# Another score bank for the softmax normalization, and activation loads issued from ScalarE's queue beside transposing DMAs, in a fused attention and feed-forward layer

## The reference, cut to what matters

```python
xn = layernorm(x)
qkv = xn @ w_in + b_in;  q, k, v = split into 16 heads
scores = q @ k.T / 8 + alibi_bias          # slope per head, causal
out = softmax(scores) @ v @ w_out + b_out
# feed-forward with quantized activations (127 / max|row|) and ternary weights
gate = silu(actq(xn) @ wq(w_gate).T);  up = actq(xn) @ wq(w_up).T
ffn  = actq(gate * up) @ wq(w_down).T
return x + out + ffn
```

## Time and profile before

| | us |
|---|---|
| timed runs, lowest / median / highest (2 runs) | 2321.36 / 2351.29 / 2381.23 |
| the profiled execution, total | 2316.97 |
| its span on the slowest core (core 0) | 2315.4 |
| spans of the eight cores | 2290.6 to 2315.4 |
| PE busy (share of the span) | 1431.2 (62%) |
| VectorE busy | 1009.0 (44%) |
| ScalarE busy | 755.1 (33%) |
| mean granted TensorE clock, core 0 | 0.775 |

### The profile page before, as it was taken

One profiled execution on the slowest core, in us unless ns is written; L12 is line 12 of the kernel. 1 busy time (PEld: TensorE's weight loads), 2 busy tenths in 40 slices (PEclk: granted clock), 3 DMA queues, 4 the chain that ended last, 5 costly groups with the idle time before them and its releaser, 6 DMA issues.

```text
span 2315.4 us, 22641 instructions; the slowest of 8 cores (2290.6 to 2315.4 us)
## 1 busy us (share of the span) xinstructions
PE 1431.2 (62%) x5304; PEld 510.8 (22%) x5304; DVE 1009.0 (44%) x1639; ACT 755.1 (33%) x1150; POOL 163.5 (7%) x276
## 2 busy tenths in 40 slices
PE   0004444466746565755657641859999999409998
PEld 0001111111211111111112110314444444204443
DVE  3005677464466763345674430215555555401110
ACT  0662222456644446756455540011221111000000
POOL 2000111100001110001110000100000000000000
PEclk9997666756657675666667665879999999759999
DMA  4764555332334453424551019781101000295661
GB/s 147 238 214 151 177 164 165 126 113 88 106 99 141 134 146 107 144 79 133 148 156 51 18 22 195 234 202 33 46 37 46 37 37 37 64 205 126 153 160 55
DMA packets 277092, 274.25 MB, mean 118 GB/s; under 512 B 208226, under 2 KB 224738, under 8 KB 276964
## 3 DMA queue, kind: packets, MB, share of 16 engines
q1 hardware_dynamic: 256740, 205.68, 34.9%
q0 software_dynamic: 20224, 67.12, 7.7%
HBM read 155.32 MB, written 67.11 MB: 96 GB/s over the span
## 4 chain that ended last, share of the span: by engine, by line
PE 42%; DVE 22%; DMA 10%; ACT 9%; issue 8%; SPq 6%; DVEq 1%; POOL 0%; ACTq 0%; POOLq 0%
PE pb L914 9%; PE pb L831 8%; PE pb L809 8%; DVE fa L529 7%; ACT ba L583 6%; SPq L189 6%; PE pb L448 5%; PE pb L503 4%; DMA fa<-w_gate 3%; DVE ba L770 3%; PE pb L570 2%; DMA s_acc<-fa 2%; DVE ba L730 2%; DVE ba L732 2%; DVE ba L735 2%
## 5 line engine op out<-in xcount | busy, mean ns | idle before, releaser
L583 ACT ACTIVATE ba<-pb,fa 128x512 bf16<-128x512 f32 (+2 forms) x522 | 338.9, 649 | 261.7 <-PE pb L570 217.8
L503 PE MATMUL pb<-ba 128*65 128x512 bf16 x502 | 232.1, 556 | 178.2 <-DVE ba L597 128.5
L759 PE MATMUL pb<-ba 128*128 128x512 bf16 x256 | 92.1, 525 | 298.9 <-DVE ba L360 173.3
L914 PE MATMUL pb<-ba 128*128 128x512 bf16 x992 | 221.2, 381 | 84.7 <-DMA ba<-s_n 84.7
L529 DVE RECIPROCAL fa<-fa 1x512 f32<-1x512 f32 x64 | 213.8, 3341 | 49.7 <-ACT fa L524 44.4
L570 PE MATMUL pb<-ba 64*128 64x512 bf16 (+2 forms) x502 | 134.7, 503 | 158.7 <-DVE ba L544 157.6
L831 PE MATMUL pb<-ba 128*128 128x512 bf16 x896 | 215.7, 381 | 23.0 <-DMA ba<-s_mu 23.0
L809 PE MATMUL pb<-ba 128*128 128x512 bf16 x896 | 216.3, 382 | 9.6 <-DVE fa L795 9.6
L819 ACT ACTIVATE fa<-pb,fa 128x512 f32<-128x512 f32 x128 | 87.9, 687 | 363.1 <-PE pb L813 363.1
L841 DVE SCALAR_TENSOR_TENSOR fa<-pb,fa 128x512 f32<-128x512 f32 x128 | 96.1, 751 | 157.9 <-PE pb L835 157.5
L914 PEld LDWEIGHTS pb<-ba 128*128 128x128 bf16 x992 | 97.5, 98 | 203.4 <-issue 87.6
(11 more groups left out here) (101 smaller groups left out, 1321.2 us busy)
## 6 DMA issues: line engine op xcount, KB each, us to landing
fa<-w_gate SPq DMA_DIRECT2D x64, 512.0 KB, 5.1
fa<-w_up SPq DMA_DIRECT2D x64, 512.0 KB, 3.9
fa<-w_down SPq DMA_DIRECT2D x64, 512.0 KB, 4.2
fa<-x SPq DMA_DIRECT2D x48, 512.0 KB, 6.1
s_n<-ba POOLq DMA_DIRECT2D x32, 512.0 KB, 2.9
fa<-w_in SPq DMA_DIRECT2D x24, 512.0 KB, 6.7
s_mg<-ba POOLq DMA_DIRECT2D x32, 256.0 KB, 5.3
s_mu<-ba POOLq DMA_DIRECT2D x32, 256.0 KB, 4.3
```

Of the source, the lines that this page charges most:

```text
L503: g = B.op("tensor", lambda e, ob=B.P[obank], k=ki2, hh=h2, pb=pbuf2, f1=first, l1=lastk: e.matmul(ob[0:65, :], v_sb[:, 1040 * k + 65 * hh ...
L583: eg.append(B.op("scalar", lambda e, b=Sb, q=qg0, g0=gw, a=wlo, c=col, pb=pbuf, jj=j: e.activation(out=pb[:, q - 512 * jj:q - 512 * jj + g ...
L759: B.em("tensor", lambda e, b=Pb, cc=c, t=ts_, hh=half: e.matmul(b[:], xn_fm[cc][:, 128 * t:128 * t + 128], wv_sb[:, 1024 * cc + 512 * hh:1 ...
L914: B.em("tensor", lambda e, b=Pb, cc=c, lt=tl, hh=half, nf=n2f: e.matmul(b[:], nf[cc][:, 128 * lt:128 * lt + 128], md[cc][:, 512 * hh:512 * ...
```

## The change

There are three parts.

1. `part2` takes the third bank of the head's pool (4 or 7) and no longer the first (2 or 5).
2. In the output projection the 16 loads of x are issued from ScalarE's queue, with the same gates. In the down projection the 16 loads of `s_acc` are, too.
3. In the down projection the first transpose of `s_n2` is issued before that of `s_md`. That of `s_md` is split into chunks 0 to 15 and 16 to 31, and PE waits for the second only before the 17th matmul of the first half tile.

```diff
@@ part2 @@
-                        rbank = SPOOL[loc3][0]
+                        rbank = SPOOL[loc3][2]
@@ ph_outproj @@
-            dv = B.dma("sync", xt[par], xv[t], "LX%d" % par, gate=ld_guard[par])
+            dv = B.dma("scalar", xt[par], xv[t], "LX%d" % par, gate=ld_guard[par])
@@ ph_ffn_down @@
-        dtr = B.dma("sync", md_all.rearrange("p (c t) -> p c t", c=NO),
-              B.s_md.rearrange("t (c p) -> t c p", c=NO), "DTR", transpose=True,
-              gate=B.gateup_tail + B.mdone.get("d", []) + t_f2 + s_f2)
-        B.waitg("tensor", [dtr])
...
         load_n2(0)
+        dtr_gate = B.gateup_tail + B.mdone.get("d", []) + t_f2 + s_f2
+        dtr_a = B.dma("sync", md_all.rearrange("p (c t) -> p c t", c=NO)[:, 0:16, :],
+                      B.s_md.rearrange("t (c p) -> t c p", c=NO)[:, 0:16, :], "DTR",
+                      transpose=True, gate=dtr_gate)
+        dtr_b = B.dma("sync", md_all.rearrange("p (c t) -> p c t", c=NO)[:, 16:32, :],
+                      B.s_md.rearrange("t (c p) -> t c p", c=NO)[:, 16:32, :], "DTR2",
+                      transpose=True)
+        B.waitg("tensor", [dtr_a])
...
-                dv = B.dma("sync", acc[par], av[t], "LA%d" % par, gate=ld_guard[par])
+                dv = B.dma("scalar", acc[par], av[t], "LA%d" % par, gate=ld_guard[par])
...
                     for c in range(NO - 1):
+                        if tg_ == 0 and tl == 0 and half == 0 and c == 16:
+                            B.waitg("tensor", [dtr_b])
```

## The result

The changed kernel takes 2306.9 us (median of 28 runs, 2275.9 to 2409.9) against 2317.1 us for the kernel before beside it (27 runs). The ratio is 0.9915, 95% interval 0.9896 to 0.9935: faster by 0.85%, less than the 2% that counts as a change, and outside the forecast range (2240, 2205 to 2292). The profiled execution took 2292.4 us, its slowest core 2290.8 us. Executions in which the cores of one die show a lower granted clock than the others are left out of the ratios, which is why 0.9915 is not 2306.9 / 2317.1, and of such a profile only the other die's cores are read; without them the changed kernel's median is about 2298, still outside the range.

What follows compares the result with a forecast made beforehand. Bounded by feed-forward matmuls, by waits among PE, ACT and DVE in the attention, and by transposing DMAs in the holes. 2317 - 40 (bank) - 36 (x loads) - 2 (down projection) = 2239, say 2240 us; range 2205 to 2292.

Steps and rivals of the forecast that it cites:

- The check on L570's waits: Attention: PE's score matmul waits for the normalization's multiply (L544) should fall from 157.6 us to roughly 110.
- Rival 2: Attention: the bank change gives nothing, as DVE's backlog fills the moved waits; total 2279 us, chance 0.11.
- step (a): Output projection's tile loop: two tiles per cycle, 11.9 us with a 9.7 us store landing; 8 cycles end at 1483.
- step (b): Output projection's DMA engines: 32 plain transfers cost the transposes 1.2 us each, 38 in all; end 1488 to 1489, gain 36.
- Rival 1: Output projection: ACT's loads get through only after the transposes are handed over; total 2275 us, chance 0.17.
- Rival 3: Output projection: loads cost the transposes nothing, both hide in each other; total 2215 us, chance 0.12.
- Rival 4: Output projection: transposes break down among 4 KB rows, 6 us per transfer; total 2389 us, slower, chance 0.05.
- SP held over 120 us by the two: Output projection: the transposes of s_n and s_mg holding SP over 120 us would show rival 4.
- the step: Down projection: s_acc loads beside the last s_n2 store delay the transposes up to 2.5 us, taken as 1.5.
- PE's two waits for s_md: Down projection: PE starts about 2060, does 16 matmuls, idles 15 us, then waits for s_md's second half until 2081.
- the second wait: Down projection: PE's second wait at L914 ends within 2 us of the old distance from the last s_n2 store.
- slices 24 and 36: Profile page's slices: the two places where TensorE was read as low, outside the feed-forward matmuls and the attention.

Runs made afterwards that it cites:

- e1_bank: Kernel before with only the normalization's move to bank 2 of the pool, all loads staying on SP's queue: 2272.3 us, ratio 0.9812.
- i0_before_one: Kernel before, unchanged, launched on one core alone instead of eight: 2257.5 us in one execution.
- e4_bank_down: Changed kernel with only the output projection's x loads put back on SP's queue: 2272.0 us, ratio 0.981.
- i1_one_core: Changed kernel launched on one core alone instead of eight: 2209.9 us in one execution.
- k2_two_halves: Changed kernel with each x load and s_acc store of the output projection issued as two half-row transfers: 2279.9 and 2291.5 us, too few for a ratio.
- h1_four_cores: Changed kernel launched on cores 0, 2, 4 and 6 alone instead of all eight: 2291.4 us.
- h2_x_later_sp: Changed kernel with x loaded and added in the down projection, s_acc and x loads on SP's queue, second s_n2 transpose behind two tiles' loads: 2232.9 us, ratio 0.9616.

## Why the prediction was wrong

**Part 1: right.** Taken 40 us; measured 41.3 in the changed kernel, and 1.9% or 43.6 us in e1_bank, with signs and places as worked out. The check on L570's waits (roughly 110) was too low, 123.7; the rest of the gain came from waits behind it (L503's for L597), which the prediction didn't list. Rival 2 falls.

**Part 2, step (a): right about the cycle.** DVE's adds on core 5, the tile pairs 13 us apart where 11.9 were forecast:

```profile
1416.79 1.48 DVE L669 TENSOR_TENSOR fa<-fa,pb 128x512 f32<-128x512 f32 x2 [10.69 <-DMA s_acc<-fa]
...
1429.88 1.48 DVE L669 TENSOR_TENSOR fa<-fa,pb 128x512 f32<-128x512 f32 x2 [9.59 <-DMA s_acc<-fa]
```

**Part 2, step (b): the step that failed**, "So a transfer costs the transposes 1.2 us; 32 of them [...] cost 38". It was mis-sized in three ways. The 1.2 us came from one store beside one transpose; with all of them there a store costs 1.7 and a load 2.2. On the quick cores that comes to 55 us instead of 38: the transposes hold SP 116 us instead of 103, and the output projection takes 122 instead of 107 (143 - 36), a gain of 14 against the mean of before. Second, one lone transfer couldn't show what both kinds do in full density on two neighbouring cores: in most pairs one of the two falls, here by a further 57 us on average. Why is open. Third, the sum was made for one core as if it stood for eight; the time is that of the worst of them.

**Rivals.** Rival 1 (loads starve) falls: x landed in 10.8 and 17.7 us beside the transposes. Rival 3 (both free) falls on every core. Rival 4 had the mechanism: its sign, "SP held over 120 us by the two", is there on cores 1, 2, 4 and 7 at 167.5 to 179.6. Its price was (173.1 - 61) / 32 = 3.5 us per transfer on these, averaged over all 32, just short of the 3.75 from which it decides, and far from the 6 it was worked out with. It deserved more than 0.05: the only row against it was a single store.

The Trainium skill's rule that was weighed, that spreading DMAs over issuing engines saves only issuing time ("DMA: Bandwidth & Descriptors", section "Issuing engines are not separate DMA queues"), gave 2275 for a part 2 worth nothing. Without part 2 the kernel takes 2272.0, and with it 24 us more. The rule warned in the right direction; that moving the issue may cost is what the runs add.

The Trainium skill's page "HBM Reference", section "Specifications (TRN2)", says that two cores share a memory domain's bandwidth, and that a DMA-bound change is to be measured with the pair active. The advice agrees with i0_before_one (8 MB in 29.6 us alone, 38.1 to 43.6 with the neighbour). Its rate of about 358 GB/s per core was reached by none of the stretches with transposes that were read here (279 GB/s the most, on one core alone), and the parted cores 4 and 5 moved 385 to 416 together, so a limit at that rate is not what they ran into.

**Part 3: right in being small**, 2 us forecast, +0.2% of time measured alone and nothing beside part 1 (e4_bank_down against e1_bank). The last s_n2 store landed late, as the step said, but by more. PE's two waits for s_md came as described, but closer together (10.0 us idle between them, where 15 was worked out):

```profile
2002.59 0.53 POOL L191 DMA_DIRECT2D s_n<-ba  x1 [5.04 <-DVE fa L877]
...
2010.40 15.28 SPq L189 DMA_TRANSPOSE ba<-s_n  x1
2025.97 30.86 SPq L189 DMA_TRANSPOSE ba<-s_md  x2
2043.23 5.80 PE L920 MATMUL pb<-ba 128*128 128x512 bf16 x15 [57.35 <-DMA ba<-s_md]
2059.05 6.20 PE L920 MATMUL pb<-ba 128*128 128x512 bf16 x15 [10.02 <-DMA ba<-s_md]
```

The transposes start 7.8 us after the store's issue; before it was 2016.60 - 2012.43 = 4.2, so 3.6 lost where 1.5 was taken. One sign was wrong: the second wait should have ended within 2 us of the old distance from the last s_n2 store (2081.13 - 2012.43 = 68.7), and ended 2059.05 - 2002.59 = 56.5 us after it, 12 us sooner. The next paragraph has the reason.

**What gave part of it back.** The down projection is 281.1 us in the changed kernel and 292.5 in e4_bank_down, with the same code from the barrier on. In the changed kernel the spans of a pair's cores up to it differ by some 50 to 70 us, and the first 12 MB of its transposes hold SP 15.28 + 30.86 = 46 us (46 to 48 on all eight cores), as on a lone core (14.89 + 31.04 = 45.9 in i1_one_core); where the cores reach it about together, in e4_bank_down, they take 54 to 62, the most on core 0:

```profile
1974.28 20.21 SPq L189 DMA_TRANSPOSE ba<-s_n  x1
1994.78 41.91 SPq L189 DMA_TRANSPOSE ba<-s_md  x2
```

That the distance in time is the cause fits i0_before_one (down projection 282.2 without a neighbour), and k2_two_halves shows it within one execution of one kernel: its parted pairs 2/3 and 4/5 hold SP 46 to 48 us there and have a down projection of 280.8 to 282.7, its other two pairs 54 to 61 and 288.9 to 299.1. It wasn't tried by itself. So a pair that doesn't part gains little over the whole kernel: in the 16 executions of the changed kernel, the mean span of a pair's two cores is 2257.9 us where they differ by 45 us or more and 2263.6 where they differ by under 26. What the parting costs is that the time is that of the slower one. For the slowest cores of the two profiles, core 4 after and core 0 before, the account closes: attention -45.3, output projection +41.6 (185.0 against 143.4), gate and up -2.5, down -18.4, together -24.6 = 2290.8 - 2315.4.

**Open.** What the neighbours share, why the fall mostly takes one core and not both, and why the fallen core stays slow (190 GB/s) at a time when its neighbour, if they started together, has gone quiet. Which core's transposes begin earlier doesn't decide it: in the eight parted pairs of the changed kernel, h1_four_cores and k2_two_halves it was the earlier one that fell in four. One core of every pair alone wasn't to be had by launching on part of the cores. The 1.7 and 2.2 us are means over eight cores in kernels that also differ in when the transfers are issued. The prediction's slices 24 and 36 are counted differently: from 0, the low ones are 24 and 35.

## What to carry to other kernels

Before plain transfers are moved beside a bulk transpose, take the price of each kind, load and store, from a place as dense as the planned one and with the neighbouring core in the same phase, and read it on the slowest core; here a single transfer (1.2 us) showed less than what the dense case came to. Where a stage is bound by its DMA engines, take bytes out of it to a stage with room, as h2_x_later_sp does with x (3.8% against before), rather than lay them over each other, and try the loads in line with the transposes in one queue where PE waits for the next transpose. And open the list of cores first: cores that part in a pattern point to a thing shared in pairs, which the page of the slowest core can't show.

## What the runs showed of the hardware

- With the neighbour at work, a core transposes 8 MB in 38.1 to 43.6 us (the kernel before on eight cores), alone in 29.6 us (one execution).
- Beside transposes, a 512 KB store that GpSimd issues costs them 1.7 us and a 512 KB load that ScalarE issues 2.2 us; on a lone core the mean is 2.1 us. Half the bytes per row cost about a quarter less (1.3 for 1.8, and 1.5 for 2.1 on a lone core).
- With both kinds in full, one core of a pair can fall to 121 to 142 GB/s while the other moves 264 to 274, and hold its transposes 48 to 68 us longer (85 in one pair); in another pair of the same run neither falls. The share of DMA time is about 1.2 on both and doesn't show it.
- Transposes of 12 MB take 46 to 48 us where the neighbour reaches them some 50 to 70 us earlier or later, and 54 to 62 where the two reach them about together.
